# The masked q of a routed linear-attention block: made by VectorE in one operation, or by GpSimd in two

## Time and profile before

| what | us |
|---|---|
| median of 3 runs | 1115.26 |
| lowest and highest | 1110.68, 1119.51 |
| profiled execution: its span | 1185.4 |
| attention in it, about | 150 to 722 |

### The profile page before, as it was taken

How to read it: one execution, slowest core, us unless ns; L and a number is a source line. 1 busy time by engine, 2 the same in 40 slices (tenths; PEclk the granted TensorE clock), 3 DMA queues, 4 the chain that set the end, 5 groups by cost and what they waited for, 6 DMA issues and landing times.

```text
span 1185.4 us, 26150 instructions
## 1 busy us (share of the span) xinstructions
PE 1044.6 (88%) x8982; PEld 766.7 (65%) x8982; DVE 901.3 (76%) x2067; ACT 643.1 (54%) x1580; POOL 519.2 (44%) x480
## 2 busy tenths in 40 slices
PE   4775788889998898999999997989998899899997
PEld 3553556656676665666766665767776677677774
DVE  3785577789995677778878787788888887886764
ACT  2432444445564555766657554756666566555564
POOL 2216144431324443222232126767886554465552
PEclk9798899999998999999999899999999899999999
DMA  8994233332333332222222116331532233225230
GB/s 231 399 343 102 72 98 113 106 97 87 107 103 96 92 102 80 72 69 69 71 75 70 49 37 178 92 96 27 152 101 63 65 96 107 54 78 151 80 90 18
DMA packets 85504, 124.16 MB, mean 105 GB/s; under 512 B 11264, under 2 KB 68096, under 8 KB 81280
## 3 DMA queue, kind: packets, MB, share of 16 engines
q1 hardware_dynamic: 75136, 97.30, 27.4%
q0 software_dynamic: 10240, 25.18, 7.5%
HBM read 71.32 MB, written 51.13 MB: 103 GB/s over the span
## 4 chain that ended last, share of the span: by engine, by line
PE 57%; DVE 21%; ACT 9%; issue 7%; another core or an unknown queue 4%; SPq 0%; DMA 0%; POOL 0%; DVEq 0%; ACTq 0%; POOLq 0%
PE wide L1437 7%; PE bank L1412 7%; PE bank L1497 6%; PE bank L1699 5%; PE bank L1689 5%; PE wide L1689 5%; DVE epp L1775 4%; PE bank L1481 4%; DVE kvw L1782 3%; PE bank L1489 2%; PE bank L1426 2%; DVE att L1539 2%; PE bank L1399 2%; ACT epp L1750 1%
## 5 line engine op out<-in xcount | busy, mean ns | idle before, releaser
L1652 POOL TENSOR_TENSOR kvw<-kvw,hq 128x512 f32<-128x512 f32 x128 | 171.7, 1341 | 150.5 <-ACT kvw L1742 150.3
L907 POOL DMA_INDIRECT gst<-attended_rows,idxs x128 | 136.7, 1068 | 211.5 <-DVE att L1539 107.5
L1539 DVE SCALAR_TENSOR_TENSOR att<-reach,endrel,wide 128x1024 f32<-128x1024 f32 x152 | 194.5, 1279 | 37.7 <-PE wide L1437 20.9
L258 POOL DMA_INDIRECT routed_rows<-hq,idxs x128 | 127.7, 998 | 216.3 <-DVE att L1539 108.0
L1775 DVE TENSOR_TENSOR epp<-kvw,epp 128x512 fp32r<-128x512 f32 x160 | 144.4, 903 | 77.7 <-ACT epp L1750 75.5
L1699 PE MATMUL bank<-epp,w2p 128*128 128x512 f32 x480 | 163.2, 449 | 7.0 <-DVE epp L1775 6.7
L1750 ACT ACTIVATE epp<-kvw 128x512 fp32r<-128x512 f32 x160 | 100.7, 630 | 95.6 <-DVE kvw L1782 91.3
L1689 PE MATMUL bank<-hp,w1p 128*128 128x512 f32 x480 | 139.8, 400 | 0.0
L1689 PE MATMUL wide<-hp,w3p 128*128 128x512 f32 x480 | 137.6, 395 | 0.0
L1412 PE MATMUL bank<-kvw,turned 128*128 x304 | 132.4, 518 | 3.7 <-ACT turned L1302 1.6
L1437 PE MATMUL wide<-turned,kx 32*128 32x128 f32 x2432 | 113.8, 300 | 18.6 <-DVE att L1539 12.7
(11 more groups left out here) (267 smaller groups left out, 1876.3 us busy)
## 6 DMA issues: line engine op xcount, KB each, us to landing
hq<-weight_rows SPq DMA_DIRECT2D x16, 2048.0 KB
rows<-routed_rows SPq DMA_DIRECT2D x76, 256.0 KB
routed_rows<-zero SPq DMA_DIRECT2D x2, 7168.0 KB, 33.2
attended_rows<-ob SPq DMA_DIRECT2D x76, 128.0 KB
routed_rows<-zero SPq DMA_DIRECT2D x1, 5120.0 KB, 16.6
out<-fin SPq DMA_DIRECT2D x16, 256.0 KB, 2.5
routed_rows<-hq,idxs POOLq DMA_INDIRECT x128
gst<-attended_rows,idxs POOLq DMA_INDIRECT x128
```

Of the source, the lines that this page charges most:

```text
L258: pool.indirect_dma_start(hs[s], bass.IndirectOffsetOnAxis(idxs[:, t, k:k + 1], 0), hq[:, t, :], None, bounds_check=BLOCKS[s] * P - 1, oob ...
L907: pool.indirect_dma_start(gst[:, u, k, :], None, orow[s], bass.IndirectOffsetOnAxis(idxs[:, t, k % TOPA:k % TOPA + 1], 0), bounds_check=BL ...
L1539: dve.scalar_tensor_tensor(out=att[:, n % 2, :, :], in0=reach[:, :, :].rearrange("p a c -> p (a c)").unsqueeze(1) .to_broadcast([P, 4, 2 * ...
L1652: pool.tensor_tensor(g, g, rows_of(1 - b % 2, n, n + 1), ALU.mult).then_inc(s_eu, 1)
```

## The change

`mask_q` leaves DVE's loop and becomes two operations of GpSimd: a comparison that writes 0 or 1 into `qm`, and a product of `qm` with q in place. Between them GpSimd waits for its own first result. They stand at the head of iteration n of GpSimd's loop, for block n+2, ahead of its wait for `s_a` and of its transfers.

```
+        s_lv = sem("live_positions")
...
     def attention_gpsimd(pool):
...
+            def mask_q(n):
+
+                if n in C0:
+                    pool.wait_ge(s_tab, C0.index(n) + 1)
+                pool.wait_ge(s_te, n // 2 + 1)
+                if n >= 4:
+                    pool.wait_ge(s_o, n - 3)
+                pool.tensor_scalar(qm[:, n % 4, :], column[:, :], erel[:, n:n + 1], None,
+                                   ALU.is_lt).then_inc(s_lv, 1)
+                pool.wait_ge(s_lv, n + 1)
+                pool.tensor_tensor(qm[:, n % 4, :], qm[:, n % 4, :], turned[:, n // 2 % 3, 1, n % 2, :],
+                                   ALU.mult).then_inc(s_qm, 1)
+
             for n in ITERATIONS:
+                if is_block(n + 2):
+                    mask_q(n + 2)
                 if n > 0:
                     pool.wait_ge(s_a, n)
                 post_pool(pool, n)
                 scatters(n)
...
     def attention_vector(dve):
...
-            def mask_q(n):
-                dve.wait_ge(s_te, n // 2 + 1)
-                if n >= 4:
-                    dve.wait_ge(s_o, n - 3)
-                dve.scalar_tensor_tensor(out=qm[:, n % 4, :], in0=column[:, :], scalar=erel[:, n:n + 1],
-                                         in1=turned[:, n // 2 % 3, 1, n % 2, :], op0=ALU.is_lt,
-                                         op1=ALU.mult).then_inc(s_qm, 1)
-
...
                 if is_block(n + 1):
                     mask_scores(n + 1)
-                if is_block(n + 2):
-                    mask_q(n + 2)
                 if is_block(n + 5):
                     k_features(n + 5)
```

## The result

The changed kernel takes 1121.76 us (median of 20 runs, 1118.0 to 1129.9), the kernel before 1113.91 us (20 runs, 1109.8 to 1121.5): 1.0082 times the time, 95% interval [1.0061, 1.0103], about 9 us more (7.9 between the medians; the ratios in this document compare runs made beside each other and differ from those of the medians by up to 0.2%). The forecast was 1113.0, so 2.4 us less. The measured time lies in the range of 1098 to 1129, but it moved the other way, and the second rival (GpSimd becomes the bound in rounds with two transfers) is what happened, in one of its two places.

What follows compares the result with a forecast made beforehand. PE was taken as the bound, busy 516.6 of 569.6 us in the attention. Terms -4 + 1.5 + 0 gave -2.5 us profiled, -2.4 timed: 1112.9, said as 1113 us, range 1098 to 1129.

Steps and rivals of the forecast that it cites:

- the second rival: Attention rounds with two transfers: POOL becomes the bound, +22 us less 4 from DVE, 1132 us; chance 0.15.
- What leaves DVE: Attention: 152 mask operations of 347 ns leave DVE, which shortens PE's waits for the scores mask; 4 us off.
- What POOL gets: Attention: POOL's comparison and product cost 0.9 us a block, hidden, so PE never waits for masked q; 0 us.
- The lead: Attention: q of block n+2 is masked two and a half rounds or more before PE wants it, some 8 us.
- The rival's other place: Second group's scatters: with c = 1.6, POOL loses 0.67 us in each of 26 rounds, 17 us.
- What POOL does to DVE: Attention: POOL's operations hold DVE's with two SBUF inputs, 5 rounds at 0.3 us; 1.5 us added, bounds 0 and 10.5.
- Where the transfers move: Attention's scatters and gathers: holds of PE's signals move within its round; 0 us taken, between 10 off and 18 added.

Runs made afterwards that it cites:

- the product alone: Changed kernel with the comparison left out, so GpSimd only multiplies q by the column vector; 1111.74 us, ratio 0.9984 to the kernel before.
- the first execution: The kernel before, unchanged, in the profiled execution that the prediction used; span 1185.4 us.
- the second: The kernel before, unchanged, profiled once more with the first experiments; 1111.54 us, span 1109.8 us.
- the run with blocks 60 to 89 alone: Changed kernel with GpSimd masking q of blocks 60 to 89 only, DVE all others; 1124.44 us, ratio 1.0115 to the kernel before.

## Why the prediction was wrong

**"What leaves DVE", -4 us: right.** Without the operation and with nothing put elsewhere the kernel gains 4.5 us (ratio 0.9960). The prediction said that PE's wait on the scores mask would go from 12.7 to 8 us or so; it went to 8.7. The size is shown within 1.2 to 7.7 us only, and the wait is not what shows it (12.8 us with the product alone).

**"What POOL gets", 0 us: the step that failed.** It failed by its price. The comparison was set at 0.30 us, from the affine select, "since the select has its size"; the upper bound of 0.61, the cast, was the right row:

```profile
L1262 POOL TENSOR_SCALAR hq<-column,erel x152: 593/615/1025, 132.1 to 645.3; 128x128 f32<-128x128 f32 x152
L1265 POOL TENSOR_TENSOR hq<-hq,turned x152: 452/457/1060, 132.8 to 646.0; 128x128 f32<-128x128 f32 x152
```

The product at 0.457 (0.50 predicted) was close. With what lies between them, c is 1.25 us in a round instead of 0.9.

The lead was right in size: "some 8 us" were 8.7 to 10.6 at the start of the scatters and 9.1 at block 62. What the prediction didn't do is to set it against the rounds. A mask that comes in every round takes from the lead in each heavy round and gives some back in each light one, so the 8 us cover it only if one batch's six heavy rounds take less than that and the four light ones give it back. At 1.25 us a round they take 7.7 and give back 2.0, and the second batch finds 3.4 us: PE waits 9.8 us for q in place of 0.

Would a mask of 0.9 us have been hidden, as the prediction said? No run has one. An estimate from the rows above, with 0.35 us less in each round: the first batch takes 5.6 of 9.1 us, 3.4 come back, the second takes 5.4 and 3.5 come back, and the two heaviest rounds of the third, with which the scatters end, take 5.3 us where 5.0 are left. So the lead would have lasted almost to the end, and the product alone, at some 0.4 us a round, leaves 5.4 us or more. By this estimate the price is what decided, and the conclusion at 0.9 us was near the edge and right by luck rather than by its argument.

The prediction had this mechanism as its second rival, with 0.6 us in each of 22 rounds of iterations 60 to 82, 13 us, less a lead spent once; the stretch shows 10.3 to 10.9. That these are near each other is partly chance: only 5.8 of the 10.3 are idle time of PE, and the rest is PE busy longer, mostly at a lower clock, which the rival had not.

**The rival's other place was wrong.** It charged the second group's scatters 17 us, with a threshold of c = 0.93 that came from 4.00 us a round. That pace was the first execution's alone. PE's real round there is 3.24 us, and yet blocks 0 to 30 cost only 1.8 us more (GpSimd's masks there alone: ratio 1.0017). A round with two scatters takes POOL 3.77 us (the comparisons at 173.10 and 176.87), so it loses half a microsecond in each, not the 0.67 of the rival, and regains 0.7 in the few with one scatter. The lead falls from 8.6 us at block 10 to 0.1 at block 25, and the last scatter is made at 234.35, three blocks later: the stretch ends just when it would begin to cost. With a comparison more the lead is gone at block 13 and the stretch costs 21 us (118.0 against 97.0).

**"What POOL does to DVE", +1.5: right in sign, small.** In the changed kernel `sum_state` keeps its median of 352 ns, with a longest of 1140, as predicted. Its mean goes from 369 to 371 ns, but the fair comparison is the run in which nobody makes the mask, where it is 353 (behind DVE's own mask this operation takes 0.40 us, as in the earlier trace rows): 18 ns in the mean, and six of the 152 take over 0.5 us, where none does without POOL's operations. In the run in which DVE also keeps its mask 4.2 us are spread outside of blocks 60 to 90, within the bounds of 0 and 10.5. How much of the 4.2 comes from longer operations of DVE (busy 8.3 us more in that run) and how much from a GpSimd that is late, no run separates. In the changed kernel the relief of DVE and this cost can't be told apart either.

**"Where the transfers move", 0: its ground was not a property of the kernel.** The late signals of PE belong to the first execution, whose attention is 64 us longer than that of the second; 26 of them are PE busy longer with the same work (its granted clock is 0.93 in blocks 60 to 90, where the second has 1.00). The prediction took the 6.3% between that span and the timed runs as a scale for all terms; it should have taken it as a sign that the rows of this stretch are not to be summed. Why that one execution was so is open; no run shows it again.

**The size of the loss.** What the prediction left out even in its rival is what PE's waits cost beyond themselves. Windows of the changed kernel around the wait of 3.13 us (clock is the eighth column, before the DMA share):

```profile
410.00:414.00 4.00, 3.37 (x43) 2.31 (x42) 3.79 (x10) 1.76 (x6) 2.14 (x4) 1.00 0.42 126
414.00:417.20 3.20, 0.07 (x2) 0.04 (x1) 1.90 (x8) 1.50 (x5) 2.62 (x4) 0.95 0.39 114
417.20:420.00 2.80, 2.80 (x34) 2.00 (x34) 0.74 (x1) 0.00 (x0) 2.34 (x4) 0.50 0.09 23
420.00:423.00 3.00, 3.00 (x13) 2.23 (x10) 0.88 (x3) 0.45 (x2) 2.63 (x4) 0.50 0.09 22
423.00:426.00 3.00, 3.00 (x41) 2.14 (x41) 2.45 (x7) 1.36 (x4) 2.66 (x4) 0.88 0.36 109
```

PE was busy at a granted clock of 1.00 (2.4 GHz), stood idle from 414.06 to 417.19, and had 0.50 (1.2 GHz) until about 423.7: the sixteen score matmuls at 417.88 take 1.24 us, those at 411.13 0.73. Nearly seven microseconds at half speed are over three lost, as much as the wait. It isn't a fixed price: behind the wait of 3.15 us in the run with blocks 60 to 89 alone PE had only half as long at 0.50 (mean clock 0.88 in the 14 us from 417, against 0.76 in those from 413 here). The five waits of 0.59 to 1.40 us from 377.98 to 393.59 left the clock alone. So in blocks 60 to 90 of the changed kernel PE idles 5.8 us more and is busy 4.5 us longer, and in the run with two comparisons it is 19.4 and 13.0.

**Why one wait is 3.13 us.** POOL's timeline up to it:

```profile
405.23 1.51 POOL L907 DMA_INDIRECT gst<-attended_rows,idxs  x1 [0.42 <-issue]
407.05 1.01 POOL L907 DMA_INDIRECT gst<-attended_rows,idxs  x1 [0.30 <-issue]
408.36 1.04 POOL L258 DMA_INDIRECT routed_rows<-hq,idxs  x1 [0.30 <-issue]
409.44 0.61 POOL L1262 TENSOR_SCALAR hq<-column,erel 128x128 f32<-128x128 f32 x1
410.14 0.45 POOL L1265 TENSOR_TENSOR hq<-hq,turned 128x128 f32<-128x128 f32 x1
412.06 1.11 POOL L907 DMA_INDIRECT gst<-attended_rows,idxs  x1 [1.47 <-issue]
413.48 1.00 POOL L907 DMA_INDIRECT gst<-attended_rows,idxs  x1 [0.30 <-issue]
414.79 1.03 POOL L258 DMA_INDIRECT routed_rows<-hq,idxs  x1 [0.30 <-issue]
415.85 0.66 POOL L1262 TENSOR_SCALAR hq<-column,erel 128x128 f32<-128x128 f32 x1
416.59 0.45 POOL L1265 TENSOR_TENSOR hq<-hq,turned 128x128 f32<-128x128 f32 x1
```

These are the two rounds in which a batch's gathers come in pairs, with a scatter behind them. From comparison to comparison they take 5.8 and 6.4 us, the second with 1.47 us that the trace gives no releaser for, and the lead, 2.2 us at block 82, is gone by then (`carried` waited 0.63 us at 410.74 already). The same event stands in the run with blocks 60 to 89 alone (3.15 us at 419.59).

## What to carry to other kernels

Work that is moved to an engine with much idle time has to be added up round by round against the round of the engine that bounds the kernel: 62% busy over the span is no reserve where six rounds in a row hold a gather and a scatter. A lead of several rounds is an account: the heavy rounds draw on it, the light ones pay back. The work is hidden as long as the longest row of heavy rounds draws less than the lead and the light rounds behind it pay that back before the next; a stretch that ends in time costs nothing. Where no row shows an operation and the bounds lie on both sides of a threshold, the forecast should stand on the dearer side, and a profiled execution 6% off the timed ones isn't to be scaled but to be doubted.

## What the runs showed of the hardware that was not expected

- GpSimd's comparison of a 128x128 float32 tile with one scalar a partition takes 0.615 us (median of 152), its product of two such tiles 0.457: the operation with one tile as input is the slower one. Writing bf16 to the spare tile didn't shorten it (634 ns in the mean over 150).
- Beside these operations a scatter's descriptors take 1.061 us in the mean in the attention, against 0.985 before, for the same 96 transfers: 7.3 us more of GpSimd's time that no step of the prediction had.
- Idle stretches of TensorE of much the same length were followed by very different times at half the granted clock: 3.13 us by nearly seven microseconds; the wait of 2.8 us for a scores mask near 590 us by none in the changed kernel (mean clock 1.00 in the 14 us around it), by 3.4 us before (0.88) and by some 10 us in the run in which nobody makes the mask (0.63, wait of 2.5 us). Waits of 0.6 to 1.4 us every 3.9 us left the clock at 1.00. In these profiles it moves a stretch of the attention by some 3 us with no change in what is computed there.
